# A four-layer transformer kernel: halves of layer 0's last output, earlier selected rows, and layer 1's copies shared among engines

## The reference

```python
xn = _layernorm(x)                                   # layer 0
x = x + L0_attn(xn) + L0_ffn(xn)
# L0_attn: 16 heads, latent q and k with rotary parts (64) and plain parts (16), causal softmax, @ Wo
# L0_ffn:  gating = softmax(xn @ W_gate.T); one head of k and of v is selected per token by argmax:
k_shared = einsum('bth,bthd->btd', indicator, k)
v_shared = einsum('bth,bthd->btd', gating_top1, v)
#          then 16 heads of q attend to the one shared k and v, causal
xn = _layernorm(x)                                   # layer 1
state, action = xn @ Ws, xn @ Wa                     # 32 columns each: q and k
weights = softmax(causal(state @ action.T / sqrt(32)))
x = x + (weights @ xn) @ Wo.T + bo + L1_ffn(xn)
# L1_ffn: Hadamard transform of xn, up and gate products (1024), silu, transform, down product
```

## Time and profile before

| | us |
|---|---|
| median of three runs | 938.71 |
| lowest and highest | 936.40, 944.63 |
| the profiled execution | 942.83 |
| its span in the trace | 941.1 |
| PE busy, share of the span | 840.1, 89% |
| DVE busy | 557.4, 59% |
| ACT busy | 389.5, 41% |
| POOL busy | 228.9, 24% |

### The profile page before, as it was taken

How to read it: one execution, slowest core, us unless ns; L and a number is a source line. 1 busy time by engine, 2 the same in 40 slices (tenths; PEclk the granted TensorE clock), 3 DMA queues, 4 the chain that set the end, 5 groups by cost and what they waited for, 6 DMA issues and landing times.

```text
span 941.1 us, 12037 instructions
## 1 busy us (share of the span) xinstructions
PE 840.1 (89%) x4835; PEld 494.0 (52%) x4835; DVE 557.4 (59%) x993; ACT 389.5 (41%) x476; POOL 228.9 (24%) x208
## 2 busy tenths in 40 slices
PE   8969999889998999995889998779999889989997
PEld 4545443444344435443468884523333248889776
DVE  4965768774777577215333454487777424974552
ACT  3732435445444554652442422205556763520240
POOL 4731212421141113513101010500110226820110
PEclk9878999999999999996979998869999979999999
DMA  6572149415631850204000003849000052000001
GB/s 184 95 263 34 50 112 165 112 46 91 112 80 59 140 145 1 76 1 157 1 1 1 1 1 126 136 102 135 1 2 1 1 193 76 11 1 1 1 1 46
DMA packets 35584, 64.99 MB, mean 69 GB/s; under 512 B 6164, under 2 KB 14908, under 8 KB 35460
## 3 DMA queue, kind: packets, MB, share of 16 engines
q1 hardware_dynamic: 34952, 64.08, 29.2%
q10 hardware_dynamic: 576, 0.13, 0.1%
HBM read 44.35 MB, written 16.29 MB: 64 GB/s over the span
## 4 chain that ended last, share of the span: by engine, by line
PE 63%; DVE 20%; ACT 5%; DMA 4%; SPq 3%; issue 2%; POOL 2%; ACTq 0%; DVEq 0%; POOLq 0%
PE psD L1663 12%; PE psO L1793 11%; DVE mx L1247 10%; PE psA L1663 9%; PE psD L1738 8%; PE psA L1756 7%; PE psO L1663 7%; PE psA L1755 4%; SPq L504 3%; PE psD L1740 2%; ACT Pr L938 1%; DVE hid_low L1559 1%; PE psA L1695 1%; PE psD L1804 1%; DMA Ks<-in_c_ones4b 1%
## 5 line engine op out<-in xcount | busy, mean ns | idle before, releaser
L1247 DVE TENSOR_REDUCE mx<-psD 128x1 f32<-128x512 f32 (+3 forms) x418 | 259.2, 658 | 102.1 <-PE psD L1740 72.0
L938 ACT ACTIVATE Pr<-psA 128x1024 f32<-128x1024 f32 (+3 forms) x192 | 162.1, 866 | 177.6 <-PE psA L1756 177.0
L805 POOL TENSOR_SCALAR_AFFINE_SELECT Pr<-Pr 128x512 f32<-128x512 f32 x96 | 61.2, 637 | 402.1 <-ACT Pr L938 323.5
L943 ACT ACTIVATE Pr<-psA 128x1024 f32<-128x1024 f32 (+3 forms) x96 | 63.3, 703 | 62.8 <-PE psA L1756 62.5
L1793 PE MATMUL psO<-Pr,Vh 128*32 128x512 f32 (+3 forms) x768 | 81.0, 501 | 3.2 <-POOL Pr L805 2.6
L1755 PE MATMUL psA<-Qr,Kr 128*128 128x512 f32 (+3 forms) x192 | 75.1, 405 | 5.8 <-DMA Qr<-mrow 5.8
L1740 PE MATMUL psD<-maskq,identb 128*128 128x128 bf16 x350 | 70.6, 226 | 0.0
L1738 PE MATMUL psD<-Kg,Qs 96*128 96x512 bf16 (+3 forms) x192 | 56.1, 334 | 12.8 <-DVE mx L1247 8.2
L1756 PE MATMUL psA<-Qr,Kr 113*128 113x512 f32 (+3 forms) x192 | 66.3, 351 | 0.0
L1738 PE MATMUL psD<-Kr,Qr 80*128 80x512 bf16 (+3 forms) x166 | 53.6, 348 | 6.0 <-DVE mx L1247 3.8
L1738 PE MATMUL psD<-Ks,Qs 96*128 96x512 bf16 (+3 forms) x166 | 53.9, 353 | 4.5 <-DVE mx L1247 3.7
(11 more groups left out here) (415 smaller groups left out, 1696.3 us busy)
## 6 DMA issues: line engine op xcount, KB each, us to landing
Qr<-d_qr SPq DMA_DIRECT2D x18, 512.0 KB, 11.6
d_qr<-WB SPq DMA_DIRECT2D x9, 512.0 KB, 3.1
Pr<-d_cb SPq DMA_DIRECT2D x8, 512.0 KB, 8.5
Qs<-d_gq SPq DMA_DIRECT2D x24, 128.0 KB, 4.0
Qs<-d_q SPq DMA_DIRECT2D x24, 128.0 KB
Ks<-d_k SPq DMA_DIRECT2D x24, 128.0 KB
Qr<-d_qn SPq DMA_DIRECT2D x18, 128.0 KB, 6.9
Kr<-d_kn SPq DMA_DIRECT2D x18, 128.0 KB, 7.8
```

Of the source, the lines that this page charges most:

```text
L805: pool.affine_select(out=block_, in_=block_, pattern=[[0, GH], [1, P]], compare_op=ALU.is_ge, fill=0.0, base=0, channel_multiplier=-1).the ...
L938: act.activation(place[:, h, q0:T], src[:, q0:T], ACT.Exp, scale=score_scale(i)).then_inc(a_drained, 1)
L943: act.activation(place[:, h:h + 2, q0:T], src[:, :, q0 - HALF:HALF], ACT.Exp, scale=score_scale(i)).then_inc(a_drained, 1)
L1247: dve.tensor_reduce(mx[:, j, part, h0:h0 + nh], src, AX, ALU.max).then_inc(d_drained, 1)
```

## The change

It has three parts, in the order of the kernel.

1. The selected rows of tiles 0 to 3 (`KV_FIRST`) are made before slot (0,0), on PE straight after the maxima's transpose and ahead of its waits for the maxima's DMA, on DVE after `gates()`. Tiles 4 to 7 move to slot (0,0). `KEY_KT` goes from 2 to 1, with gq1 ahead of the shared key; `max_window` then spreads group 1's maxima over slots 1 to 4.
2. Layer 0's last output is made in halves. The first 512 columns of psO, which get nothing after key tile 3, are copied by ACT in slot (7,5), transposed by PE and added by DVE in slot (7,6). The norm is taken of four tiles at a time, before and after the second half; xn is transposed by halves of four tiles, the values of tiles 0 to 3 and the first half of q and k are made between.
3. Layer 1's copies are shared: ACT makes qk1's and Q1's first blocks and Q1's third, DVE makes the three copies of k from PSUM and K1's low part, POOL Q1's low part and both blocks of `xh_low`. ACT cuts `xh_high` after the exponentials, and loads the exponential's table early with an activation on one column.

```diff
-KV_AT = {(0, 0): range(0, NT // 2), (0, 1): range(NT // 2, NT)}
-KEY_KT = 2
+KV_FIRST = range(0, NT // 2)
+KV_AT = {(0, 0): range(NT // 2, NT)}
+KEY_KT = 1
...
-            + [("xnT1", DC), ("qk1", 1), ("v1", 2), ("xh", DC), ("s1", NT), ("gate1", FC)]
+            + [("xnT1", 1), ("v1a", 1), ("xnT1b", 1), ("qk1", 1), ("v1", 1), ("xh", DC), ("s1", NT), ("gate1", FC)]
...
@@ gpsimd
-            for cut, low, w, high_part in ((up_cut, up_low, w_up, up_high), (gt_cut, gt_low, w_gt, gt_high)):
+            def weights_low(cut, low, w, high_part):
+
                 pool.wait_ge(cut, 1)
                 for c in range(DC):
                     pool.tensor_tensor(low[:, c, :], w[:, c, :], high_part[:, c, :], ALU.subtract).then_inc(low1_ready, 1)
+
+            weights_low(up_cut, up_low, w_up, up_high)
+            pool.wait_ge(low1_ready, DC)
+            pool.wait_ge(q1_ready, 1)
+            pool.tensor_tensor(Q1[RANK:2 * RANK, :], qk1[0:RANK, :], Q1[0:RANK, :], ALU.subtract).then_inc(q1_low, 1)
+            pool.wait_ge(q1_low, 1)
+            weights_low(gt_cut, gt_low, w_gt, gt_high)
+            for c in range(DC):
+                pool.wait_ge(xh_cut, c + 1)
+                pool.tensor_tensor(xh_low[:, c, :], fT[:, c, :], xh_high[:, c, :], ALU.subtract).then_inc(xh_split, 1)
...
@@ scalar, attention
+                        if (i, kt) == (2 * NG - 1, HALF0_KT - 1):
+                            act.wait_ge(pv_done, NT * i + NT // 2)
+                            act.wait_ge(d_drained, DU[f"o{i - 1}"])
+                            act.activation(OT[:, 0:HALF], psO[:, 0:HALF], ACT.Copy).then_inc(half0_out, 1)
...
-                output(groups[-1])
+                if groups[0] == 0:
+                    std(1)
+                else:
+                    output(groups[-1])
...
@@ scalar, layer 1
             act.activation(up_high[:], w_up, ACT.Copy).then_inc(up_cut, 1)
...
+            act.wait_ge(pv_done, NT * 2 * NG)
+            act.activation(OT[:, HALF:T], psO[:, HALF:T], ACT.Copy).then_inc(o_drained, 1)
+            copy_half(xnT, 0)
+            first_values(0)
+            std(1)
+            copy_half(xnT, 1)
+            src = take()
+            q = src[0:RANK, :]
+            act.activation(qk1[0:RANK, :], q, ACT.Copy)
+            act.activation(Q1[0:RANK, :], q, ACT.Copy).then_inc(q1_ready, 1)
+            act.wait_ge(k1_ready, 1)
+            act.activation(Q1[2 * RANK:3 * RANK, :], q, ACT.Copy).then_inc(a_drained, 1)
+            first_values(1)
             act.wait_ge(w1b_in, 16 * N_W1B)
             act.activation(gt_high[:], w_gt, ACT.Copy).then_inc(gt_cut, 1)
+
+            act.activation(gam[:, 0:1], ln[:, 1, 0:1], ACT.Exp)
...
@@ vector
+                if groups[0] == 0:
+                    gates()
+                    for j in KV_FIRST:
+                        selected(j)
...
+                else:
+                    norm((0, NT // 2))
+                    outputs(groups[-1], (1,))
+                    norm((NT // 2, NT))
...
+            k = psA[RANK:2 * RANK, (A["qk1"] - 1) % 2, :]
+            dve.tensor_copy(qk1[RANK:2 * RANK, :], k)
+            dve.tensor_copy(K1[RANK:2 * RANK, :], k)
+            dve.tensor_copy(K1[0:RANK, :], k).then_inc(k1_ready, 1)
+            dve.wait_ge(k1_ready, 1)
...
@@ tensor
+                if groups[0] == 0:
+                    for j in KV_FIRST:
+                        selected_unit(j)
...
                         if (i, kt) == (0, KEY_KT):
+                            features(cols(w_qkv0, P, 2 * P), normed)
                             shared_key()
-                            features(cols(w_qkv0, P, 2 * P), normed)
...
+                        if (i, kt) == (2 * NG - 1, HALF0_KT):
+                            output_transposes(i, (0,))
...
+            values_product(2 * NG - 1, NT - 1, (0, 1))
+            transposed_half(xn, NT, 0, a_unit())
+            output_transposes(2 * NG - 1, (1,))
+            at("xnT1", f"o{2 * NG - 1}")
+            pe.wait_ge(w1b_in, 16 * N_W1B)
+            values_place = a_unit()
             pe.wait_ge(a_drained, A["xnT1"])
-            pe.wait_ge(w1b_in, 16 * N_W1B)
-            features(cols(w_sa, 0, 2 * RANK), normed)
-            value_units(normed, lambda k: w_o1[:, k, :], range(DC))
+            values1(0, values_place)
+            second, qk_place = a_unit(), a_unit()
+            features(cols(w_sa, 0, 2 * RANK), normed, halves=(0,), dst=qk_place)
+            transposed_half(xn, NT, 1, second)
+            pe.wait_ge(a_drained, A["xnT1b"])
+            features(cols(w_sa, 0, 2 * RANK), normed, halves=(1,), dst=qk_place)
+            values1(1, a_unit())
             pe.wait_ge(a_drained, A["qk1"])
-            pe.wait_ge(parts1_ready, 2)
+            pe.wait_ge(q1_low, 1)
+            pe.wait_ge(parts1_ready, 1)
```

More of the change, by code:

```diff
@@ L1055, in _ @@
                                scale=float(1.0 / np.sqrt(RANK))).then_inc(a_drained, 1)
+            for c in range(DC):
+                cut_transformed(c)
             def cut_hidden(m):
@@ L1266, in maxima_rows, with outputs @@
                                 src[0:rows, 0:P]).then_inc(d_drained, 1)
-            def outputs(i):
-                for b in range(2):
+            def outputs(i, halves=(0, 1)):
+                for b in halves:
                     src = take().rearrange("p (j h v) -> p j h v", j=4, h=GH)
@@ L1664, in product, with features @@
                 return op
-            def features(weights, rhs, chunks=None):
-                dst = a_unit()
-                for half in range(2):
+            def features(weights, rhs, chunks=None, halves=(0, 1), dst=None):
+                dst = a_unit() if dst is None else dst
+                for half in halves:
                     c = slice(half * HALF, (half + 1) * HALF)
@@ L1704, in transposed_half, with value_tiles @@
                         op = pe.transpose(dst[:, at_:at_ + P], src[:, j, c * P:(c + 1) * P], identf[:])
+                op.then_inc(a_filled, 1)
+            def value_tiles(u, dst, lhsT, rhs, chunks):
+                for j in range(4):
+                    op = product(dst[:, j * D:(j + 1) * D],
+                                 [(lhsT(k, tile_cols(4 * u + j)), rhs(k)) for k in chunks])
                 op.then_inc(a_filled, 1)
@@ L1797, in values_product, with output_transposes @@
                     op.then_inc(pv_done, 1)
-            def output_transposes(i):
-                pe.wait_ge(o_drained, i + 1)
-                for b in range(2):
+            def output_transposes(i, halves=(0, 1)):
+                if halves == (0,):
+                    pe.wait_ge(half0_out, 1)
+                else:
+                    pe.wait_ge(o_drained, i + 1)
+                for b in halves:
                     dst = d_unit()
```

59 lines of the change are left out of this document (28 added, 31 removed).

## The result

The kernel after took 934.86 us (median of 20 runs, 926.13 to 940.35), the kernel before 942.23 beside it (20 runs, 935.0 to 948.13): a ratio of 0.9917, 95% interval 0.9898 to 0.9937. A second series of the same kernel gave 0.9907 [0.9868, 0.9946]. The profiled execution has a span of 937.7 us (941.1 before). It took 939.37 us, the fifth longest of its 20, so the two profiles lie only 3.4 us apart where the medians lie 7.4 apart.

A forecast was written before the change was run, and what follows sets the result against it. PE was taken as the bound, gains coming only from its idle and low-clock time. 10.0 - 1.0 + 11.9 = 20.9 us took the profiled 942.83 to 921.9, 917.8 as median; range 911 to 927.

The forecast's parts named there:

- term M: Layer 1's entry, up to its maxima: they start 8.7 us sooner at full clock, taken as 6.5 us.
- Part A (1) to (4): Layer 0's start: selected rows early, less work behind, new waits, maxima spread over slots 1 to 4; 10.0 us gained.
- the new waits: Layer 0's start: ROPE 2 waits for the shared key, scores for gq1's copy; 1.8 us lost.
- the loss of 1.2: Layer 0's start: the scores begin 1.2 us later, behind the early selected rows.
- The rival in which DVE and PE alternate: Group 0: without overlap it gains only 4.6 us, time 922.2; chance 0.15, shared with two rivals together.
- the one by the clock over 63.84 to 122: Layer 0's start: early products with waits keep the clock at 0.50, so not faster, up to 973 us; chance 0.05.
- Part A (5): Group 2's loads, needed at slot (1,0): they move less than the work, slack 2 us; 1 us taken off.
- The rival "loads do not move": Group 2's loads stay where they were: 1.6 us less, 919.4, or 4 less if they collide, 921.8; chance 0.13.
- the rival of the entry: Clock stays down at layer 1's entry and drops again in the exponentials: 921.8 us; chance 0.17.
- Exponentials: ACT's chain before layer 1's exponentials: cuts go behind them, table load early, less idle time; 4.0 us gained.
- The value product (1.4): Layer 1's product with the values: PE's 3.6 us hole goes, clock stays up; 2.8 us counted half, 1.4.
- both rivals at 925: Group 2's loads do not move and the clock stays down in layer 1: 925 us; two rivals together share 0.15.

The follow-up runs named there:

- part A alone: The kernel before with only selected rows 0 to 3 moved early and group 1's maxima spread over more slots; 938.9 us, ratio 0.9974 to the kernel before.
- b_only: The kernel after with the selected rows and group 1's maxima left as in the kernel before; 936.86 us, ratio 0.9950 to the kernel before.
- b_mended: b_only with POOL's up_low held until four xn tiles are out, second root and second half's transposes issued earlier; 935.67 us, ratio 0.9956.
- std_early: The kernel after with ACT's second root ahead of first_values(0) and the second half's transposes ahead of the first half's query and key products; 926.16 us, 0.9823.
- best_nofill: The kernel after with the edits of best except its filling products; 923.3 us, ratio 0.9825 to the kernel before.
- lean: The kernel after with layer 1's copies cut differently: K's low part straight from PSUM on DVE, Q's copies on ACT; 931.81 us, ratio 0.9875.
- after_again: The kernel after once more, unchanged; 930.38 us, ratio 0.9907 to the kernel before.
- pool_wait: The kernel after with POOL's up_low held until the first four tiles of xn are made; 931.33 us, ratio 0.9884 to the kernel before.
- best: The kernel after with gather behind group 2's loads, filling products, up_low held, second root earlier, K's low part from PSUM; 928.0 us, ratio 0.9866.
- order: The kernel after with the gather of selected rows 12 to 15 issued behind group 2's loads; 929.76 us, ratio 0.9853 to the kernel before.

## Why the prediction was wrong

**How far each part fell short.** By the ratios part A alone was worth 2.4 us where 9.0 were forecast (its interval goes from 5.1 us down to nothing), and part B alone 4.7 where 11.9 were (1.7 to 7.7). Together that is 7.1, close to the 7.8 of the kernel after. So two steps failed, by about the same amount: what was taken off for the loads (5), and the size of term M with the exponentials behind it.

**Part A (1) to (4): the mechanism right, the size in part luck.** 10.0 us by the sum, 10.0 from the first to the second `mneg`. Its terms can be checked one by one: the new waits are 1.9 us in the profile after against 1.8, and PE's waits for the maxima fell from 3.5 us (ten) to 1.8 (four). PE has work where the gap was and the clock is 1.00 there, as the signs asked; the scores start 6.9 us behind the first `mneg`, before 6.4, so the loss of 1.2 was 0.5. The rival in which DVE and PE alternate gave 4.6 and fell, and so did the one by the clock over 63.84 to 122. But the gap of 5.83 us and the half clock up to 76 us that the sum starts from are those of one execution. Against b_only's and b_mended's profiles the same part is worth 7.3 and 6.6, and the mean of the three with the old order less the mean of the thirteen with the new one is 7.6.

**Part A (5): the first step that failed.** It asked when the loads of group 2 land and whether the products wait for them, and took 1 us off. No product waited for them. What was not asked is who else needs the DMA engines then: the maxima row of group 1, a small transfer that every group needs at once, goes out behind the loads. In before there were 8.3 us between the last load's issue (127.34) and the row; counted from the first `mneg`, part A pulled the row forward by 9.9 us and the loads by 4.5, since the gather ahead of them came only 3.2 sooner. That left 2.9 us. In place of the 1 us taken off, the cost is 2.0 us with the clock kept (1.2 in std_early, whose wait was shorter) and 6.7 to 7.7 with it lost. Over the seven profiles with this order, four of which lost it, the mean is 4.8; seven are too few to tell which is the commoner. The rival "loads do not move" had the place right and the mechanism wrong.

**Part B, term M (6.5 us, 8.7 at full clock): the second step that failed, 2.5 to 3.0.** These are the kernel after's two profiles against the one of before. The entry took 81.9, 81.5 and 79.6 us in the three profiles with the old order and 78.1 to 79.7 in the six with the new one, so by the means it is 2.1. Four sizes were off. xn: 0.34 us a tile was read where POOL stood still; in halves it meets up_low, 2 us for one tile. The clock: values(0) 5.89 and 5.49, and 4.60 to 5.95 in the other four profiles with this entry, not 3.72: the rival of the entry (the hole before the transposes is 3.29 us where 2.9 was written, and it was then taken that the loss is 2.8 of work only). The root: 4.16 us behind first_values where 2.5 was the limit. K's low part: 1.86, not 1.21, since Q's low part on POOL runs beside it. The three PSUM copies were right (1.22 against 1.2). The 8.7 at full clock was in reach, but not with this order: best_nofill, with its three edits at the entry and in an execution that kept its clock there, has 9.0 less than before (72.9 against 81.9).

"GPSIMD Engine Reference" (Key points) of the Trainium skill, which says that POOL and VectorE contend for shared SBUF interfaces, had been priced at 1.2 us for one pair and left out, because the earlier trace rows showed no slower POOL. The trace now agrees with the page, and the loser is VectorE: the earlier trace rows had looked at the wrong engine's duration. It is 2 us on xn and 0.65 on K's low part, the pair that was priced. The prediction took from the page only the instructions with two SBUF inputs, as K's low part and the add of x. The page also names those in a 2-port mode; xn's instruction has one tensor input and was held all the same, and which mode it runs in no run shows.

**Exponentials (4.0): 2.6 and 1.4 in the two profiles of after, 4.3 in `lean`.** The table load left the chain as forecast. The term holds where PE keeps its clock; after the wait of 2.15 us ahead of the maxima it runs at 0.50 from 458 to 460 us, and PE in place of ACT is late. *The value product (1.4):* from 474.35 to 492.17 it took 17.8 us in the kernel after instead of 18.7, and 18.7 in after_again: 0.9 or nothing, not the 16 to 17 us asked for.

**The sum against its own time.** It is made against one execution. Where no instruction differs the profiles lie up to 2.2 us apart ("to 7"), and 5.6 in the rest, which no edit touches behind the value product. By an estimate from these two spreads and the one of group 0 (67.8 to 71.1), a forecast from one profile carries about 3 us either way; the range should have had it. Where the prediction puts the time with both rivals at 925, its own terms give 923.4 (1.6 and 4.0 more than 917.8) or 925.8 (4 and 4.0).

## What to carry to other kernels

When work moves forward, list every transfer that will be under way beside its own, in whichever queue, not only those it feeds: ask of each small, urgent DMA what will stand ahead of it in the new order. When two engines will newly run side by side on SBUF, the durations read where one of them stood still are lower bounds; hold the patient one back with a wait. Filling products are no free insurance: where the wait was gone they cost their own 2 us, and at the entry they delayed the chain. And compare more than one profile of the kernel before: one execution's wait and clock can be 3 us of a forecast.

## What the runs showed of the hardware

- The granted clock behind the same wait differs between executions of one kernel. Ahead of group 1 it fell to 0.50 behind 1.72 us (`after`) and stayed at 1.00 behind 1.95 us (`after_again`); at layer 1's entry, behind 3.29 us in both, it was 0.50 in the first and 1.00 in the second. What decides it no run settled. Ahead of group 1 it stayed down for some 16 us although PE was then busy 7.86 of 8.00 us (138 to 146 us, had shown 6 us of work).
- While POOL subtracts with 1024 columns, some of DVE's instructions stand still until the running subtraction is over, and are out 0.2 to 0.3 us behind its end: one `xn` tile of 0.34 us took 2.44 (`lean`; shown by pool_wait's edit), an add of x of 0.42 took 2.26 in pool_wait and b_mended, 2.42 in `best` and 1.00 in best_nofill, by where in POOL's instruction it fell (seen in four timelines, not edited away by itself). Others do not: statistics of x took 1.40 us for four beside POOL in best_nofill, as with POOL idle (1.41 in the kernel after), and a copy from PSUM took 1.22 beside Q's low part.
- The row of maxima (`Qs<-mrowb`, 8 KB) was there only 5.8 to 6.0 us after its issue in the two profiles of the kernel after, behind 1.5 MB that another queue had been given in the 7.2 us before; with the DMA engines empty (`order`) PE did not wait for it.
